# Half of each expert's low up weights made on GpSimd, at the head of a tick

## What is computed

```
# layer 0: 16 experts, top 4, hidden 512
weights = zeros.at[topi].set(softmax(topv))
a   = silu(einsum('bsd,edh->bseh', h, w1)) * einsum('bsd,edh->bseh', h, w3)
y   = einsum('bseh,ehd->bsed', a, w2)
out = x + einsum('bsed,bse->bsd', y, weights)
# layer 1: 16 experts, top 6 of a softmax, hidden 352, plus a shared expert
gate_up = einsum('th,eoh->teo', xf, w1);  act = silu(g) * u
moe_out = einsum('te,tei,ehi->th', combine, act, w2)
```

## Time and profile before

| | |
|---|---|
| median of 3 runs | 2888.7 us (2884.29 to 2888.86) |
| profiled execution | 2881.25 us, span 2879.5 us |
| PE busy | 2598.8 us (90%) |
| VectorE (DVE) busy | 1715.9 us (60%) |
| ScalarE (ACT) busy | 1131.5 us (39%) |
| GpSimd (POOL) busy | 776.9 us (27%) |
| low parts of the up weights, L806 | 127.7 us on VectorE, x128 |
| granted TensorE clock | 0.946 over the span |

### The profile page before, as it was taken

One profiled execution on the slowest core, in us unless ns is written; L12 is line 12 of the kernel. 1 busy time (PEld: TensorE's weight loads), 2 busy tenths in 40 slices (PEclk: granted clock), 3 DMA queues, 4 the chain that ended last, 5 costly groups with the idle time before them and its releaser, 6 DMA issues. The chain is left out here.

```text
span 2879.5 us, 50247 instructions
## 1 busy us (share of the span) xinstructions
PE 2598.8 (90%) x15563; PEld 2138.3 (74%) x15564; DVE 1715.9 (60%) x3327; ACT 1131.5 (39%) x2434; POOL 776.9 (27%) x792
## 2 busy tenths in 40 slices
PE   7989879979799989799996798998999999699997
PEld 6878757768688877578775686776777788688886
DVE  4525847659777656567674456865444426566664
ACT  1102336533243324445452123655445431344443
POOL 3203200004333225423333200650000012255554
PEclk9999979999899979899998799999999989899999
DMA  4534122214631145477773242444212031566663
GB/s 161 160 119 118 30 78 72 68 39 150 174 103 52 30 135 177 125 217 217 199 215 89 82 93 50 149 129 144 72 62 72 21 116 41 162 160 159 160 159 68
DMA packets 289189, 332.99 MB, mean 116 GB/s; under 512 B 147349, under 2 KB 202597, under 8 KB 287216
## 3 DMA queue, kind: packets, MB, share of 16 engines
q1 hardware_dynamic: 217808, 252.57, 28.1%
q0 software_dynamic: 20640, 51.74, 9.2%
q10 hardware_dynamic: 50560, 26.34, 3.1%
HBM read 233.86 MB, written 96.72 MB: 115 GB/s over the span
## 5 line engine op out<-in xcount | busy, mean ns | idle before, releaser
L875 PE MATMUL e_psum<-e_up_hi,hT_hi 128*128 x672 | 245.7, 366 | 21.0 <-DVE hT_lo L843 15.5
L876 PE MATMUL e_psum<-e_up_lo,hT_hi 128*128 x672 | 237.7, 354 | 0.0
L877 PE MATMUL e_psum<-e_up_hi,hT_lo 128*128 x672 | 237.4, 353 | 0.0
L875 PEld LDWEIGHTS e_psum<-e_up_hi,hT_hi 128*128 128x128 f32 x672 | 127.5, 190 | 43.3 <-issue 30.6
L1473 POOL TENSOR_TENSOR self_a_p<-self_a_p,self_a_mx 112x448 f32<-112x448 f32 x96 | 96.1, 1002 | 215.4 <-DVE self_a_mx L1530 215.4
L772 ACT ACTIVATE e_gate<-e_psum 128x352 f32<-128x352 f32 (+1 forms) x86 | 44.5, 517 | 257.2 <-PE e_psum L877 256.8
L849 DVE TENSOR_TENSOR hT_lo<-e_psum,hT_hi 128x256 fp32r<-128x256 f32 (+2 forms) x138 | 55.7, 435 | 146.2 <-ACT hT_hi L790 137.3
L1564 ACT ACTIVATE self_a_p<-self_a_p 112x448 f32<-112x448 f32 x128 | 71.7, 575 | 180.7 <-POOL self_a_p L1473 126.2
L877 PEld LDWEIGHTS e_psum<-e_up_hi,hT_lo 128*128 128x128 f32 x672 | 127.5, 190 | 12.3
L876 PEld LDWEIGHTS e_psum<-e_up_lo,hT_hi 128*128 128x128 f32 x672 | 127.7, 190 | 10.6
L1694 PEld LDWEIGHTS joint_psum<-x_v,joint_a_pt 125*112 125x112 f32 (+1 forms) x1024 | 119.5, 178 | 19.9 <-issue 14.0
(11 more groups left out here) (559 smaller groups left out, 7374.0 us busy)
## 6 DMA issues: line engine op xcount, KB each, us to landing
e_up_raw<-in_L_ffn_w SPq DMA_DIRECT2D x64, 512.0 KB, 8.5
e_up_raw<-in_L_ffn_w SPq DMA_DIRECT2D x64, 352.0 KB
e_dn_raw<-in_L_ffn_w SPq DMA_DIRECT2D x16, 1024.0 KB, 15.1
q_all<-p_p_t_stage ACTq DMA_DIRECT2D x56, 256.0 KB
e_dn_raw<-in_L_ffn_w SPq DMA_DIRECT2D x16, 512.0 KB
x_q<-q_all SPq DMA_DIRECT2D x8, 896.0 KB
k_ctx<-front_c_t_stage SPq DMA_DIRECT2D x32, 187.5 KB, 2.4
v_ctx<-front_c_v_stage SPq DMA_DIRECT2D x24, 250.0 KB
```

The costliest lines, as they stand in the source:

```text
L875: pe.matmul(out, lhs[0], rhs[0], start=k == 0, stop=False)
L876: pe.matmul(out, lhs[0], rhs[1], start=False, stop=False)
L877: return pe.matmul(out, lhs[1], rhs[0], start=False, stop=k == n_k - 1)
```

## The change

VectorE keeps pieces 0 and 1 of each expert and makes them at the end of the due tick, as before. Pieces 2 and 3 are made by GpSimd, at the head of its next tick, ahead of that tick's gather and add. Each engine counts on a semaphore of its own (`up_ready[0]`, `up_ready[1]`, 2 per expert); PE and SyncE wait on the one that belongs to their piece. For the first expert, VectorE and GpSimd each make their half at the head of tick -1.

```diff
-        up_hi_ready, up_ready, dn_hi_ready, dn_ready = (...)
+        up_hi_ready, dn_hi_ready, dn_ready = (...)
+        up_ready = s.sems("up_ready", 2)
+        HK = KC // 2
@@ sync
-                    reuse(sp, up_ready, (e - 1) * KC + k + 1)
+                    reuse(sp, up_ready[k // HK], (e - 1) * HK + k % HK + 1)
@@ gpsimd
+            def split_up(e, slot):
+                for k in range(HK, KC):
+                    pool.wait_ge(up_hi_ready, e * KC + k + 1)
+                    pool.tensor_tensor(up_lo[:, bass.ds(slot * KC + k, 1), :], up_raw[:, k:k + 1, :],
+                                       up_hi[:, bass.ds(slot * KC + k, 1), :].bitcast(F32), ALU.subtract).then_inc(up_ready[1], 1)
+
             def tick(j, u, item, now):
+                if isinstance(j, int) and j == -1:
+                    split_up(0, 0)
+                if item(-1) is not None:
+                    with pool.If(now.due_before != 0):
+                        split_up(now.e_before + 1, (now.e_before + 1) % 2)
                 i = item(2)
@@ vector
-            def split_up(e, slot, pieces):
-                for k in pieces:
+            def split_up(e, slot):
+                for k in range(HK):
...
-                                      ... ALU.subtract).then_inc(up_ready, 1)
+                                      ... ALU.subtract).then_inc(up_ready[0], 1)
@@ vector tick
-                    split_up(0, 0, range(KC))
-                if item(-1) is not None:
-                    with dve.If(now.due_before != 0):
-                        split_up(now.e_before + 1, (now.e_before + 1) % 2, range(KC // 2, KC))
+                    split_up(0, 0)
...
-                        split_up(e + 1, (e + 1) % 2, range(KC // 2))
+                        split_up(e + 1, (e + 1) % 2)
@@ tensor
-                            pe.wait_ge(up_ready, e * KC + k + 1)
+                            pe.wait_ge(up_ready[k // HK], e * HK + k % HK + 1)
```

More of the change, by code:

```diff
@@ L639, in routed_expert_stage @@
         up_in, dn_in, next_in = s.sems("up_in", KC), s.sems("dn_in", 2), s.sem("next_in")
-        up_hi_ready, up_ready, dn_hi_ready, dn_ready = (s.sem(n) for n in ("up_hi_ready", "up_ready", "dn_hi_ready", "dn_ready"))
+        up_hi_ready, dn_hi_ready, dn_ready = (s.sem(n) for n in ("up_hi_ready", "dn_hi_ready", "dn_ready"))
+        up_ready = s.sems("up_ready", 2)
+        HK = KC // 2
         made, dve_order, onehot_ready, listed, idx_ready, h_transposed, h_hi_ready, h_ready = (
@@ L801, in _ @@
             order = Order(dve, dve_order)
-            def split_up(e, slot, pieces):
-                for k in pieces:
+            def split_up(e, slot):
+                for k in range(HK):
                     dve.wait_ge(up_hi_ready, e * KC + k + 1)
                     dve.tensor_tensor(up_lo[:, bass.ds(slot * KC + k, 1), :], up_raw[:, k:k + 1, :],
-                                      up_hi[:, bass.ds(slot * KC + k, 1), :].bitcast(F32), ALU.subtract).then_inc(up_ready, 1)
+                                      up_hi[:, bass.ds(slot * KC + k, 1), :].bitcast(F32), ALU.subtract).then_inc(up_ready[0], 1)
             def split_down(e, slot):
```

## The result

The changed kernel takes 2908.55 us (median of 4 runs, 2905.78 to 2912.69), the kernel before 2887.02 us (4 runs, 2884.29 to 2888.86): ratio 1.0081, 95% interval 1.0068 to 1.0094. It is slower by 21.5 us, where I had forecast 2896, 7.4 us more. The time lies in the range (2872 to 2913), but the sum is three times too small.

What follows compares the result with a forecast made beforehand. PE was taken as busy nine tenths or more, its waits 33 us (3.5 first stage, 30 second) capping any gain. First stage -3.5 and second +10.9 gave +7.4 on 2888.7, so 2896 us, range 2872 to 2913.

Steps and rivals of the forecast that it cites:

- D becomes a plain tick, -0.9 us per expert: Second stage, PE tick at whose head an expert's weights are split: VectorE's shorter chain takes it from 7.93 to 7.02 us.
- GpSimd's pieces take 1.69 and 2.38 us and wait for VectorE's pair: GpSimd's subtractions of 704 and 1024; in the second stage they start at 4.2, after VectorE's pair, and end at 7.4.
- Free experts, D + A = 15.5: Second stage, weight-split tick plus the next, add not held: gather 1.05 us late; 15.5 against 15.8, a gain of 0.3.
- the term of 0.4: Tick after the weight split: a late row transpose also pushes the down products behind it, 0.4 us added.
- Held experts, D + A = 17.7, 7 of 15: Second stage, add held through VectorE's chain: gather lands 3.2 us late; both ticks 17.7 against 15.8, a loss of 1.9.
- Sum of the second stage, +10.9: Second stage: 8 experts at -0.3 us and 7 at +1.9 us, +10.9 us.
- The first expert's pieces cost nothing: Ahead of the first stage: they lie beside the first gather's landing, no cost; without that cover at most 8 us.
- The next weights, nothing: SyncE's loads start later as raw pieces free 0.8 and 1.6 us later; no ScalarE wait, nothing, otherwise below 1 us.
- The port was not shared (2856): Rival: GpSimd's subtractions share the port, gather stays in place, nearly all 33 us come back, 2856; chance 0.05.
- VectorE was not held at `e_back` (2924): Rival: GpSimd's piece holds VectorE's one-element copy ahead of e_idx and hT_lo; +35 us, 2924; chance 0.10.
- 2881: Rival: GpSimd's add is no longer held behind VectorE's chain; 15 x -0.3 - 3.5 = -8 us, 2881; chance 0.22.
- 2870: Rival: add not held and the gather lands in 2.7 us; -18.5 us, 2870; chance 0.10.

Runs made afterwards that it cites:

- the kernel with one-element pieces: The changed kernel with both GpSimd subtractions cut to one element in the ticks of the loop, low parts left out for later experts; 2882.8 us.
- the gap: The changed kernel with a one-element write by VectorE ahead of each of its two pieces, in both stages; 2911.1 us.

## Why the forecast was right in sign and small in size

- *D becomes a plain tick, -0.9 us per expert.* Right: D is 7.02 to 7.35 us in 13 of 15 experts, 9.69 in the first and 8.05 in the third (7.70 to 8.29 before, 9.40 in the first), `e_act_raw` at 4.8, hT_lo's wait 2.0 us. The first stage's -3.5 came as -2.5.
- *GpSimd's pieces take 1.69 and 2.38 us and wait for VectorE's pair.* Right: 1.72 and 2.43 unhindered (means in the kernel with the pieces behind the gather), ends at 7.4 in free ticks and 9.1 in held ones, gathers to 8.7 and 10.9 where I had 8.9 and 10.5.
- *Free experts, D + A = 15.5.* The failed step. Measured 16.25. PE waited 0.57 us on average for the landing, where I had taken 1.05; mis-sized is the term of 0.4 for what a late transpose pushes on, the only other one that I had for A. A is 9.02 us, 2.0 more than a plain tick, so that term was 1.4. What I had meant by it is there, in its size: in all 14 A ticks in which PE waited, the first down product starts 0.77 to 0.83 us behind the transposes, and 0.39 in every other kind of tick. The other 1.0 stands further back in A: the down products take up to 0.3 us longer, PE idles 0.2 to 0.9 us ahead of the transposes of the activation in four of these eight ticks, which the profile puts down to its own issue, and in six the next tick's first product stands 0.8 behind them in place of some 0.4. That part does not need a late gather. An A tick of the kernel before in which PE waits for no row, 2646.21 to 2654.98:

```profile
2646.21 0.43 PE L875 MATMUL e_psum<-e_up_hi,hT_hi 128*128 x1 [0.47 <-issue]
...
2650.50 0.66 PE L919 MATMUL e_psum<-ident,e_rows 128*128 128x128 f32 x4
...
2654.14 0.54 PE L885 MATMUL e_psum<-ident,e_act_raw 128*128 128x128 f32 x3 [0.47 <-issue]
2654.98 0.42 PE L875 MATMUL e_psum<-e_up_hi,hT_hi 128*128 x1 [0.29 <-issue]
```

  It takes 8.77 us, two more of that kind take 8.41 and 8.35, and three in the kernel with one-element pieces 8.31 to 8.52. So already the reading of the kernel before was wrong: I had put A's 0.8 us over a plain tick down to GpSimd's late gather, and PE's waits for it are 2.0 us in all there, 0.13 per expert. What makes these ticks long stays open.
- *Held experts, D + A = 17.7, 7 of 15.* Right in kind. There were 6, at 17.4 to 19.2 (mean of 5, without the last, 18.4). Missing was a second hold, by the one-hot of A: the gather's issue ends 1.8 us behind the second piece in place of 1.3. The gathers of these ticks landed 3.4 us after their end, less than the 4.06 I took, so PE's wait came out at 2.9 in place of 3.2. Again A holds more than the wait and 0.4: 0.9 us on average, part of it the clock, 0.84 to 0.89 in four of the six A ticks.
- *Sum of the second stage, +10.9.* Measured +17.1 in the profile of the changed kernel and +23.2 in that of the kernel with the change there alone; 366.0 us before, and 366.9 where the stage was left as it was. Free experts account for 8 x (16.25 - 15.8), held ones for 6 x (18.4 - 15.8), together some 19. Of the 8 us by which these parts miss the forecast (-2.4 and +13.3), 6 are the free experts.
- *The first expert's pieces cost nothing.* Wrong by 2.2 us (the head, 37.0 against 34.8). They did not lie beside the landing alone. VectorE and GpSimd alternate on the first stage's first pieces:

```profile
1225.03 4.53 DVE L819 TENSOR_TENSOR e_up_lo<-e_up_raw,e_up_hi 128x1024 fp32r<-128x1024 f32 x2
1226.11 5.64 POOL L729 TENSOR_TENSOR e_up_lo<-e_up_raw,e_up_hi 128x1024 fp32r<-128x1024 f32 x2
...
1232.90 2.86 POOL L746 DMA_INDIRECT e_rows<-h_rows,e_idx  x1
...
1241.06 0.66 PE L929 MATMUL e_psum<-ident,e_rows 128*128 128x128 f32 x4 [1.28 <-DMA e_rows<-h_rows,e_idx]
```

  The second gather, issued at 1224.70 in the kernel before (1.2 us ahead of PE's first product), came 1.2 us behind it here and took 2.86 us, and PE waited 1.28.
- *The next weights, nothing.* Wrong as to the reason. ScalarE never waits for them, but their packets stand beside the gather. In the experiments the first piece came with 0.66 us more of landing (free experts).
- *The rivals.* The port was not shared (2856), and VectorE was not held at `e_back` (2924), which took 0.15 us in the two D ticks above. The add is still held, so 2881 and 2870 fell too. A page's rule stood behind the rival of 2881: by the Trainium skill (SBUF — State Buffer, section "SBUF: two separate sides") the pair of ports is held "for the whole instruction". The trace differs in one respect, in both directions: the add waited through the one-hot and both pieces (4.21 us), and VectorE's piece through both of GpSimd's (4.88 us). Instructions of the holder that follow each other directly behave as one hold here, and with a pause between them (the gap) the waiting engine gets in more often than not.

## What to carry to other kernels

Before work goes to an engine that is idle 73% of the time, look at what stands behind it in that engine's queue, and at whose work it holds at the shared port: here the same two pieces cost 1 us per expert ahead of the gather and as much behind it, and a single piece behind it gained 0.5. A transfer issued earlier need not land earlier by as much when weight loads are under way beside it; read the landing in the trace, and whether a moved piece also frees the buffer later that the loads wait for. And a tick can grow by more than PE's wait in it: A was 4.2 us over a plain tick with a mean wait of 2.89 us, and 2.0 over with 0.57. Before such an excess is put down to the wait, look for ticks of the same place that waited for nothing; here some of them were 1.3 to 1.8 us over too.

## What the runs showed of the hardware that I had not expected

- Beside two plain subtractions of GpSimd a VectorE subtraction with two SBUF inputs took 4.88 us in place of 0.9. Beside VectorE's one-hot and pieces the issue of an indirect DMA on GpSimd took 4.2 us (two pieces, changed), 5.0 (three) and 5.8 (four) in place of 1.6, 0.8 us more for each piece.
- A one-element write of 0.06 us between two VectorE operations let the add in 4 times out of 6 (2.61 us).
- An indirect gather of 128 rows lands 2.3 to 3.4 us after its end where no weight loads follow, 2.5 to 4.9 with them beside it, and 6.8 in the worst place.
- The mean granted clock of TensorE was 0.86 over an A tick with a wait of 3.24 us, against 1.00 in plain ticks, and over the first two ticks of the first stage it was 0.78 and 0.75 with waits of 2.03 and 1.46 us ahead of them, against 0.85 and 1.00 before with 2.04 and 1.02. 1.00 is the upper of its two levels, 2.4 GHz; a mean below it holds time at 1.2 GHz.
